# Half-by-half attention and first expert, with the residual added by VectorE, in a fused attention and mixture-of-experts kernel

## What is computed

```python
x = x + tanh(g_xattn) * xattn(layernorm(x), ctx)
x = x + tanh(g_ffn)   * ffn(layernorm(x))

def xattn(query, key):                 # query: x, 56 tokens; key = value: the first 56 of ctx
    Q, K, V = projections, split into 16 heads
    corr = irfft(rfft(Q) * conj(rfft(K)))          # circular correlation over the tokens
    w, idx = top_k(corr.mean(-1), 4)               # per head: 4 best shifts
    out = sum_k softmax(w)[k] * roll(V, idx[k])
    return out @ Wo + bo

def ffn(x):                            # x: 896 tokens
    logits = x @ Wr + br               # 8 experts; softmax over the best two, the others 0
    h = gelu(x @ W1[e] + b1[e])        # for every expert e
    return sum_e weights[:, e] * (h @ W2[e] + b2[e])
```

## Time and profile before

| | |
|---|---|
| median of 3 runs | 133.5 us (132.34 to 134.25) |
| the profiled execution | 132.46 us, of which the span from its first to its last instruction is 130.2 us |
| mean granted TensorE clock | 0.956 of full |
| PE, PEld busy | 117.5 us (90%), 94.7 us (73%) |
| DVE, ACT, POOL busy | 89.9 us (69%), 80.5 us (62%), 62.9 us (48%) |
| the chain that ended last | PE 70%, DVE 14%, ACT 5%, issue 5%, POOL 2% |

### The profile page before, as it was taken

How to read it: one execution, slowest core, us unless ns; L and a number is a source line. 1 busy time by engine, 2 the same in 40 slices (tenths; PEclk the granted TensorE clock), 3 DMA queues, 4 the chain that set the end, 5 groups by cost and what they waited for, 6 DMA issues and landing times.

```text
span 130.2 us, 1685 instructions
## 1 busy us (share of the span) xinstructions
PE 117.5 (90%) x575; PEld 94.7 (73%) x575; DVE 89.9 (69%) x175; ACT 80.5 (62%) x107; POOL 62.9 (48%) x50
## 2 busy tenths in 40 slices
PE   6999969998878993959999999999999999999950
PEld 2397555544465891939999999999999999999930
DVE  1583687529386498999679877775775775775991
ACT  3027764401355755928878878878878878878900
POOL 0001460005203999999999999980330330330802
PEclk9999995559999999999999999999999999999998
DMA  3896000000310215400891340030040030000003
GB/s 93 234 406 249 0 0 5 3 0 0 101 60 0 82 79 161 162 6 9 238 337 43 107 146 0 0 141 0 0 141 3 5 141 0 0 0 0 0 0 141
DMA packets 3833, 10.07 MB, mean 77 GB/s; under 512 B 697, under 2 KB 1066, under 8 KB 3826
## 3 DMA queue, kind: packets, MB, share of 16 engines
q1 hardware_dynamic: 3154, 9.43, 21.5%
q10 hardware_dynamic: 672, 0.55, 1.5%
HBM read 9.49 MB, written 0.49 MB: 77 GB/s over the span
## 4 chain that ended last, share of the span: by engine, by line
PE 70%; DVE 14%; ACT 5%; issue 5%; POOL 2%; POOLq 1%; DVEq 0%
PE bank L772 23%; PE bank L799 22%; PE bank L641 7%; PE bank L658 3%; ACT prod L409 3%; POOL cf L329 2%; DVE hidl L617 2%; PE bank L664 2%; ACT hidh L416 2%; DVE prod L496 2%; DVE tw L496 2%; PE bank L718 2%; PE bank L735 1%; DVE qk L261 1%; PE bank L748 1%
## 5 line engine op out<-in xcount | busy, mean ns | idle before, releaser
L617 DVE TENSOR_TENSOR hidl<-prod,hidh 128x896 fp32r<-128x896 f32 (+1 forms) x34 | 45.3, 1339 | 19.8 <-ACT hidh L416 19.8
L409 ACT ACTIVATE prod<-bank,col_sb 128x896 f32<-128x896 f32 (+1 forms) x34 | 32.9, 967 | 14.5 <-PE bank L772 11.8
L323 POOL TENSOR_TENSOR wel<-we_sb,weh 128x512 fp32r<-128x512 f32 x16 | 25.6, 1604 | 20.9 <-issue 19.9
L416 ACT CAST hidh<-prod 128x896 fp32r<-128x896 f32 (+1 forms) x34 | 30.5, 899 | 1.0
L329 POOL TENSOR_TENSOR cf<-cf,kf 128x448 f32<-128x448 f32 x12 | 17.9, 1496 | 26.6 <-DVE kf L604 26.4
L799 PE MATMUL bank<-hidl,weh 128*128 128x448 f32 x64 | 18.5, 368 | 2.2 <-DVE hidl L617 2.2
L772 PE MATMUL bank<-xth,weh 128*128 128x448 f32 x64 | 18.6, 366 | 0.3 <-ACT xth L404 0.3
L772 PE MATMUL bank<-xtl,weh 128*128 128x448 f32 x64 | 18.6, 367 | 0.0
L772 PE MATMUL bank<-xth,wel 128*128 128x448 f32 x64 | 18.5, 365 | 0.0
L799 PE MATMUL bank<-hidh,weh 128*128 128x448 f32 x64 | 18.4, 367 | 0.0
L799 PE MATMUL bank<-hidh,wel 128*128 128x448 f32 x64 | 18.3, 365 | 0.0
(11 more groups left out here) (118 smaller groups left out, 116.7 us busy)
## 6 DMA issues: line engine op xcount, KB each, us to landing
we_sb<-in_w_experts SPq DMA_DIRECT2D x8, 512.0 KB, 5.0
route_b<-route_scratch SPq DMA_DIRECT2D x8, 448.0 KB, 3.6
out<-vf SPq DMA_DIRECT2D x2, 224.0 KB, 1.9
tb<-in_tab_b SPq DMA_DIRECT2D x1, 297.0 KB, 6.3
ta_c<-in_tab_ctx SPq DMA_DIRECT2D x1, 274.8 KB, 4.9
wa_sb<-in_w_attn SPq DMA_DIRECT2D x1, 256.0 KB, 5.7
x_sb<-in_x SPq DMA_DIRECT2D x1, 224.0 KB, 3.8
x_sb<-in_x ACTq DMA_DIRECT2D x1, 224.0 KB, 4.1
```

The costliest lines, as they stand in the source:

```text
L323: gp.tensor_tensor(wel[:, e, k, :], we_sb[:, e % RING, k, :], weh[:, e, k, :].bitcast(F32), ALU.subtract).then_inc(we_split, 1)
L409: act.activation(hid[:, n % 2, halves, :], bank[:, 2 * (n % 2):2 * (n % 2) + 2, 0:TOK][:, halves, :], ACT.Gelu, bias=col_sb[:, P_B1 + n:P_ ...
L416: act.copy(hidh[:, n % SLOTS, halves, :], hid[:, n % 2, halves, :]).then_inc(hid_hi, 1)
L617: ve.tensor_tensor(hidl[:, n % SLOTS, halves, :], hid[:, n % 2, halves, :], hidh[:, n % SLOTS, halves, :].bitcast(F32), ALU.subtract).then ...
```

## The change

1. **Residual.** `add_residual` (two identity products on PE) and ACT's copy to x2 go; DVE adds `xres` to PE's bank (`attended`) and takes its statistics from the sum.
2. **Halves.** PE's, ACT's and DVE's programs are rewritten so that tile t and half h of attention each follow on their own, the first ahead. The top-4 search is done for one tile at a time. The first norm and the second are done per half.
3. **1/sqrt.** Nine small DVE instructions per norm (L466 to L476) become one `pow` of 112x4 elements on POOL per half (`invert`), between DVE's variance and DVE's `shift`.
4. **Expert 0** is done in eight half chunks, four of the first half ahead, while the second half of attention is still in its norm.
5. **Fillers.** 7 and 5 at the start, none later.
6. **POOL.** Rests of experts 0 and 1 come in pieces of 128 columns, without the waits for `of` and for the second norm; the pairs of experts 2 to 7 wait for `route_ok`, which DVE gives when the expert weights are done. The additions still stand behind all pairs.
7. **Loads.** The bias rows come over POOL's queue; experts 5 to 7 are loaded from inside the loop that loads `route_b`.
8. **End.** DVE alone makes the last sum of half 1; POOL's share of 160 columns goes.

```diff
+            def invert(times, half):
+
+                tiles = slice(half * HT, (half + 1) * HT)
+                gp.wait_ge(var_ok, 2 * times + half + 1)
+                gp.tensor_tensor(rstd[:, tiles], var[:, tiles], minus_half[:, :], ALU.pow).then_inc(rstd_ok, 1)
...
-                gp.wait_ge(in_we[e], 16)
-                if e == 0:
-                    gp.wait_ge(of_ok[0], 1)
-                if e == 1:
-                    gp.wait_ge(xn_v, sum(by_vector))
...
+            for e in range(LEAD_BY_SCALAR):
+                gp.wait_ge(in_we[e], 16)
+                for k in range(2):
+                    gp.wait_ge(lead_s, 2 * e + k + 1)
+                    rest(e, k)
+            invert(1, 0)
+            invert(1, 1)
+            gp.wait_ge(route_ok, 1)
+            for e in range(LEAD_BY_SCALAR, E):
...
-            for half in range(2):
-                act.wait_ge(stat_ok, NT + HT * (half + 1))
-                act.copy(x2[:, half * HT:(half + 1) * HT, :], tiled(bank[0:PT, half, :])).then_inc(x2_ok, 1)
...
+            def attended(half):
+
+                tiles = slice(half * HT, (half + 1) * HT)
+                ve.wait_ge(xres_ok, half + 1)
+                ve.wait_ge(attn, half + 1)
+                ve.tensor_tensor(x2[:, tiles, :], tiled(bank[0:PT, half, :]), xres[:, tiles, :], ALU.add).then_inc(x2_ok, 1)
+                ve.wait_ge(x2_ok, half + 1)
...
             def take_expert(e, half):
 
-                if e < E - 1:
-                    ve.wait_ge(y_expert, HC * (e + 1))
-                    if e >= 2:
-                        ve.wait_ge(acc_ok, 2 * (e - 2) + half + 1)
-                else:
-                    ve.wait_ge(last_half, half + 1)
+                ve.wait_ge(y_expert, unit(HC * e + HC - 1, half))
+                if e >= 2:
                     ve.wait_ge(acc_ok, 2 * (e - 2) + half + 1)
                 ve.wait_ge(in_route[e], 16)
```

More of the change, by code:

```diff
@@ new lines, in _ @@
+            weights_turned(0)
+            lead(1, 0)
+            lead(1, 1)
+            exponentials(1)
+            take(v_proj, 0, vf, 0, v_ok, 1)
+            weights_turned(1)
+            act.preload_act_table(ACT.Gelu)
+            gated(0)
+            act.wait_ge(wrc_mm, 1)
+            act.copy(wrc[:, :], bank[:, 6, 0:E]).then_inc(wrc_ok, 1)
+            gated(1)
+            normalise(x2, 1, 0)
+            attended_turned(0)
+            lead_of_tokens(0)
+            attended_turned(1)
@@ L433, in _ @@
+            for n in range(HC, LAST):
+                chunk(n, BOTH)
+            chunk(LAST, HALF[0])
+            chunk(LAST, HALF[1])
         @block.vector
@@ L803, in project @@
-                if n < E * HC - 1:
-                    mm.then_inc(y_expert, 1)
-            hidden(0)
-            hidden(1)
-            for n in range(E * HC):
-                if n + 2 < E * HC:
-                    hidden(n + 2)
-                if n == 3:
-                    turn_routes()
-                project(n)
+                for k, (w, t) in enumerate(operands):
+                    pe.wait_ge(hid_ok if k == 2 else hid_hi, unit(n, last))
+                    for half in range(halves.start, halves.stop):
+                        mm = pe.matmul(bank[:, 6 - 2 * (e % 2) + half, 0:TOK], w_of(w), t[:, slot, half, :],
+                                       start=(c == 0 and k == 0), stop=(c == HC - 1 and k == 2))
@@ new lines, in project @@
+                mm.then_inc(y_expert, 1)
+            pe.wait_ge(warm_ok, 1)
+            keep_busy(FILL_FIRST, 3)
+            pe.wait_ge(dc_ok, 1)
+            pe.wait_ge(in_rows, 16)
+            for half in range(2):
+                open_projection(0, 6, half)
+                open_projection(1, 4, half)
+            keep_busy(FILL_SECOND, 3)
+            context_spectra(0)
+            context_spectra(1)
+            x_spectra(0)
+            pe.wait_ge(in_wa, 16)
+            keys(0)
+            queries(0)
@@ new lines, in _ @@
+            x_spectra(1)
+            keys(1)
+            queries(1)
+            pe.wait_ge(in_tb, 16)
+            head_sums(0)
+            values(0)
+            correlations(0)
+            head_sums(1)
+            weights_turned(0)
+            correlations(1)
+            weight_spectra(0)
+            values(1)
+            repeated(0)
+            weights_turned(1)
+            weight_spectra(1)
+            output_products(0)
+            repeated(1)
+            attention(0)
+            centred_router()
```

601 lines of the change are left out of this document (319 added, 282 removed).

## The result

The changed kernel takes **139.57 us** (median of 4 runs, 137.43 to 142.05) against 133.88 for the kernel before on the same chip; the ratio is 1.0455, 95% interval 1.0343 to 1.0568: slower. Forecast were 132.8, between 128.0 and 137.0.

What follows compares the result with a forecast made beforehand. TensorE alone was taken to bound the end; of its 7.3 us gain POOL's wait left 1.7. Span 130.2 - 1.7 + 1.2 (clock) - 0.2 (end) = 129.5, giving 132.8 us from the median, range 128.0 to 137.0.

Steps and rivals of the forecast that it cites:

- The front: Start up to the first query-key product: 13.0 instead of 14.21, gain 1.2 us, bounds 0 and 1.5; fillers hide late rows.
- rival B: Attention: clock stays up or comes back early, about 3.5 us off, total 129.3 us; chance 0.23.
- Attention at 1.2 GHz: Attention, from 13.0 to x2's start at 31.75: half clock assumed, values and repeat 1.6 us each.
- Residual: Attention's end: DVE's addition is new on the chain, +0.6 us for half 0, hidden for half 1.
- `pow` 0.6: Norm: small DVE steps of 1.8 us become a `pow` on POOL, taken as 0.6 us, bounds 0.2 and 2.85.
- Expert 0: Half chunks of expert 0, ACT setting the pace at first: expert weights done 10.9 us after 38.5, at 49.5.
- rival D: Slower: TensorE stays at 1.2 GHz until the experts begin, expert weights at 52.0, total 136.7 us; chance 0.18.
- Norm as a whole: Second norm: x2 at 32.35 after the addition, factors 34.45, first half chunk leaves PE at 38.5, 4.7 us earlier.
- POOL, the new wait: POOL's pairs start at 49.5, first addition late, DVE goes on at 80.9; TensorE idles some 4.5 us.
- rival E: Slower: POOL and DVE strictly in turn, a pair takes 3.46 us, total 136.4 us; chance 0.05.
- The clock behind the gap: After TensorE's idle time in POOL's wait: clock may fall, +1.2 us, bounds 0 and 4.
- C: POOL is never late, pairs near 1.91 us throughout, TensorE sets the end, total 126.0 us; chance 0.12.

Runs made afterwards that it cites:

- experiment 4: Additions of experts 1 and 2 moved ahead in POOL's queue, wait kept: changed kernel 128.64 us, ratio 0.978; kernel before with the wait 130.01 us, ratio 0.9806.
- experiment 6's first kernel: Changed kernel with bias rows third on SP's queue and the five fillers behind the rows left out, seven kept ahead: 135.04 us, ratio 1.0326.
- experiment 7: Kernel before with the residual alone changed (identity products and ACT's copies out, DVE's addition in): 131.93 us beside 133.34.
- experiments 5: Changed kernel, rows on SP, 13 fillers ahead: 132.19 us. Without POOL's wait, rows on SP, more loads ahead: 135.79 us; that with 13 fillers ahead: 133.09 us.
- experiment 3: Kernel before with only the wait for `route_ok` ahead of POOL's pairs and the change's load order: 137.26 us, ratio 1.0482.
- experiment 1: Changed kernel without POOL's wait for `route_ok`, so the pairs start behind the second norm: 134.98 us, ratio 1.0276.

## Why the prediction was wrong

- **The front** (step "the five fillers behind them hide a late landing by a microsecond or so", gain 1.2): here it failed. I had 13.0 for the first `prod` and bounds of 0 and 1.5 on the gain; it was 17.23, a loss of 3.0. I priced the transfer's landing and not what TensorE's waiting for it does: seven fillers, at half speed (0.45 us each), end at 4.35, TensorE idles 2.47 us, and is still at half speed through openings, fillers and most of the context products, where the kernel before, without the pause, had reached full speed by the openings (1.05 against 1.84 us). With the front put back `prod` is at 12.95, `route` ends at 50.44 where I had 49.5, and the kernel takes 132.19 where I had 132.8. Part of that agreement is luck: the gap in its trace is 6.10 us where I took 4.5, and what makes up for it isn't settled. Its executions have mean granted clocks from 0.922 to 0.961, so some of them probably ran the attention faster than I assumed, as in rival B.
- **Attention at 1.2 GHz**: right. I had 18.75 us from `prod` to x2; it took 18.53, and 18.45 with the front put back. But it took 17.05 in the trace of experiment 4 and 16.06 in that of experiment 6's first kernel, so rival B's higher clock does occur in part of the runs.
- **Residual**: +0.6, measured 0.69; alone, no loss (experiment 7).
- **`pow` 0.6**: 1.05, inside its bounds, 0.45 over my value.
- **Expert 0** (10.9 from the first half chunk to the expert weights): the first GELU at 43.80 and `route` at 57.69 make 13.9 in the profile after, but 11.3 and 10.7 in experiments 5 and 4. The term was right where the clock was up. The mechanism of rival D, TensorE at 1.2 GHz into expert 0, did occur in the profiled run; experiment 4 shows the same program of TensorE without it.
- **Norm as a whole**: from x2 to the first half chunk out of TensorE I had 6.75 us; it took 8.04. Of the 1.3 more, 0.45 are the `pow`; the rest I can't assign.
- **POOL, the new wait**: right as a mechanism, and close in size. From the first pair to the end of the addition I had 31.4 us; it took 32.7. DVE's wait was 7.1 by the forecast and 8.06 in the trace, at L629 and with L326 as releaser. I took the gap as 4.5; it is 5.91. The rate of pairs beside DVE, 2.63 us on average, fits the 2.7 and not the 3.46 of rival E.
- **The clock behind the gap** (+1.2, bounds 0 and 4): mis-sized. It had fallen before TensorE went on, and cost 2.8. I had argued from a 2.2 us hole that left the clock alone; a gap of 5.9 us did not. The Trainium skill, "TensorE: Matmul & The Clock Gate", section "Part 1: The HAM clock gate", has the array's clock drop to 1.2 GHz when idle; this trace shows it behind 5.9 us.
- **The chances**: I gave 0.35 to "faster" on B and C, both of which need TensorE or POOL to run better than the rows showed, and 0.23 to "slower". Gap and clock together are 8.7 us against a gain of 7.3 by TensorE alone: with the clock term at its upper end the sum already reached 135.6. The two late terms came out on the same side.

**The sum, station by station in the profile after** (forecast, measured): first `prod` 13.0, 17.23; x2 31.75, 35.76; first half chunk 38.5, 43.80; expert weights 49.5, 57.69; first addition done 80.9, 90.41. The addition is 9.5 us late: 4.2 by the front, -0.2 by attention, 1.3 by the norm, 2.9 by expert 0, 1.3 by POOL. With 1.6 more for the clock behind the gap that makes 11.1, and the span is 10.8 above the forecast of 129.5. So the front is the largest term, and expert 0's low clock the second. The two executions near 137.4 us lie 4.6 above the forecast of 132.8, about what the front makes; no trace of them exists, so that they ran expert 0 at full clock isn't shown.

The forecast counted a quiet POOL in expert 0 within its 7.3 us ("with POOL quiet"), but never asked what the wait alone is worth: 4.7 us there (14.36 to 9.64 in experiment 3), more than half of the whole gain.

## What to carry over

Ask of a wait that quiets a helper engine two things apart: what it frees beside it, and which of the helper's later duties slide behind it. Here moving two groups of additions ahead in the helper's queue turned a loss of 4.8% into a gain of 1.9%. And an input that lands late costs TensorE more than the wait if nothing keeps it busy meanwhile: place fillers ahead of the wait, not behind it.

## What was not expected of the hardware

- TensorE began at half speed in every trace (seven 512-column fillers 3.17 us); with 13 fillers it had full speed by the openings (1.02 to 1.13 us), with or without a pause of up to 1.1 us ahead of them. With seven fillers and 2.47 us of idle time behind them its next work was still at half speed (five fillers 2.24 us, against 1.25 with no idle time ahead), while the granted clock in the windows reads 1.00 there: at the front only durations show it. It isn't the same each time: behind 2.56 us of idle time in experiment 1 the openings took 1.02, and the half speed (clock 0.50 from 9 to 11 us) came only behind them.
- A `pow` of 112x4 on GpSimd takes 1.01 to 1.11 us, though a 512-column cast takes 0.61 alone.
- DVE's steps of 64 columns with two inputs take 0.22 to 0.29 us alone and 0.52 to 1.20 beside GpSimd's pairs, and one with a single input (`lnum`) 0.60 instead of 0.19; the long `hidl` steps (1.08 alone, 1.38 on average in the kernel before) suffer far less in proportion. In this kernel the small steps are where the sharing hurts.
- The bias rows land 5.4 to 5.7 us after their issue on GpSimd's queue and 4.2 to 4.8 us after it on SP's, in the midst of the other loads.
- The same TensorE program ran expert 0 once at clock 0.53 (40 to 51 us) and once at 1.00.
